# Mamba scan: in 8 of 16 steps VectorE adds the two states of the product and TensorE makes one identity sum instead of two

## What is computed

```python
dA = jnp.exp(delta[..., None] * -jnp.exp(a_log))
mi = ALPHA * delta[..., None] * Bm[:, :, None, :] * xb[..., None]

def scan_fn(carry, inp):
    h, v = carry
    dA_t, mi_t, C_t = inp
    v = BETA * v + mi_t
    h = dA_t * h + v
    y_t = jnp.einsum('ben,bn->be', h, C_t)
    return ((h, v), y_t)
...
y = ys.transpose(1, 0, 2) + dp * xb
y = y * jax.nn.silu(z)
return jnp.einsum('ble,de->bld', y, ow)
```

## Time and profile before

| | |
|---|---|
| median of 3 runs | 4198.9 us |
| the profiled execution, its own time | 4208.4 us |
| its span, first to last instruction | 4206.7 us |
| TensorE busy, share of the span | 3402.9 us, 81% |
| VectorE busy | 2586.9 us, 61% |
| GpSimd busy | 2097.3 us, 50% |
| ScalarE busy | 1958.7 us, 47% |
| L912 products on GpSimd, 512 | 1233.8 us, 2413 ns each |
| L1049 scans on VectorE, 512 | 1169.1 us, 2283 ns each |
| L1323 identity sums on TensorE, 2048 records | 1056.9 us |

### The profile page before, as it was taken

The page is one execution under the profiler, slowest core; times in us unless marked ns, Lnnn a source line. Parts: engine busy times, 40 slices in busy tenths (PEclk is TensorE's granted clock), DMA queues, the critical chain, the costliest instruction groups (busy, mean ns, idle before and its releaser), DMA issues. The chain is left out here.

```text
span 4206.7 us, 66615 instructions
## 1 busy us (share of the span) xinstructions
PE 3402.9 (81%) x20348; PEld 2295.0 (55%) x20349; DVE 2586.9 (61%) x3839; ACT 1958.7 (47%) x4228; POOL 2097.3 (50%) x1304
## 2 busy tenths in 40 slices
PE   6888886982899898999974998999989863799980
PEld 4455554651555555555543555555555543688870
DVE  3444442234677777777754777777777757654545
ACT  1211111212676767676734766676676733233320
POOL 0101100002677777777752877777777855321216
PEclk9888887995999999999986999999999985699995
DMA  1000000001222222222221222223232324111113
GB/s 53 0 0 0 0 0 22 0 30 53 54 67 68 65 69 63 70 63 69 63 61 32 73 63 63 71 55 81 54 80 53 79 72 168 61 45 47 47 43 109
DMA packets 151434, 227.93 MB, mean 54 GB/s; under 512 B 25108, under 2 KB 83892, under 8 KB 149558
## 3 DMA queue, kind: packets, MB, share of 16 engines
q1 hardware_dynamic: 143156, 202.30, 17.9%
q0 software_dynamic: 8064, 23.08, 1.8%
HBM read 119.99 MB, written 23.59 MB: 34 GB/s over the span
## 5 line engine op out<-in xcount | busy, mean ns | idle before, releaser
L912 POOL TENSOR_TENSOR m_hc<-m_h,m_Cb 128x1024 f32<-128x1024 f32 x512 | 1233.8, 2413 | 419.3 <-PE m_bank L1323 280.6
L1049 DVE TENSOR_TENSOR_SCAN m_h<-m_dA,m_vel 128x1024 f32<-128x1024 f32 x512 | 1169.1, 2283 | 59.4 <-ACT m_dA L1189 13.0
L1323 PE MATMUL m_bank<-m_hc,ident 128*128 128x512 f32 x2048 | 1056.9, 631 | 102.3 <-POOL m_hc L912 101.9
L1189 ACT ACTIVATE m_dA<-m_delta,m_rate 128x255 f32<-128x255 f32 x2048 | 874.0, 497 | 42.8 <-DVE m_h L1049 23.7
L1339 PE MATMUL m_vel<-m_M,m_U 128*128 128x128 bf16 x4096 | 544.9, 223 | 88.3 <-DVE m_h L1049 63.1
L1341 PE MATMUL m_vel<-m_M,m_U 112*128 112x128 bf16 x4096 | 545.1, 223 | 0.0
L1323 PEld LDWEIGHTS m_bank<-m_hc,ident 128*128 128x128 f32 x2048 | 362.4, 198 | 321.1 <-issue 221.3
L1339 PEld LDWEIGHTS m_vel<-m_M,m_U 128*128 128x128 bf16 x4096 | 403.2, 99 | 222.8 <-DVE m_h L1049 110.2
L1341 PEld LDWEIGHTS m_vel<-m_M,m_U 112*128 112x128 bf16 x4096 | 407.9, 100 | 81.0 <-issue 68.3
L1038 DVE TENSOR_TENSOR m_vel<-m_vel,m_entry 128x4 f32<-128x4 f32 x512 | 82.8, 162 | 377.1 <-PE m_vel L1341 375.3
L1253 PE MATMUL m_bank<-m_pair,m_in 128*128 128x256 f32 x1024 | 280.0, 402 | 37.6 <-DVE m_cv L989 31.8
(11 more groups left out here) (280 smaller groups left out, 5744.6 us busy)
## 6 DMA issues: line engine op xcount, KB each, us to landing
m_Cb<-m_c_rows SPq DMA_DIRECT2D x256, 256.0 KB, 3.3
m_M<-m_Mhi SPq DMA_DIRECT2D x128, 256.0 KB, 4.3
m_M<-m_Mlo SPq DMA_DIRECT2D x64, 256.0 KB, 3.9
m_U<-m_Uhi SPq DMA_DIRECT2D x128, 128.0 KB, 3.2
y_rows<-x_y SPq DMA_DIRECT2D x40, 256.0 KB, 2.1
m_U<-m_Ulo SPq DMA_DIRECT2D x64, 128.0 KB, 3.3
g_stage<-in_e_w SPq DMA_DIRECT2D x8, 1024.0 KB, 5.3
o_stage<-in_e_w SPq DMA_DIRECT2D x16, 512.0 KB, 4.4
```

Of the source, the lines that this page charges most:

```text
L912: nc.gpsimd.tensor_tensor(hc[:, g].rearrange("p m a t -> p m (a t)"), h[:, p % 2, 2 * g:2 * g + 2].rearrange("p m a t -> p m (a t)"), Cb[: ...
L1049: nc.vector.tensor_tensor_scan(flat(h), flat(dA), VB[:, 2 * g * 512:2 * (g + 1) * 512], 0.0, ALU.mult, ALU.add).then_inc(s["scan_done"], 1)
L1189: nc.scalar.activation(dA[:, p % 2, m, a, 1:CM], delta[:, par, m, 1:CM], ACT.Exp, scale=rate[:, m, NG * p + a:NG * p + a + 1]).then_inc(s[ ...
L1323: last = nc.tensor.matmul(Y[g][:], net.ident[:], hc[:, g, :, a, :], start=(p == 0 and a == 0), stop=(p == NPAIR - 1 and a == NG - 1))
```

## The change

In steps 2, 3, 4, 7, 8, 11, 12 and 13 of each chunk (`FOLDED`) VectorE adds the second state's half of `hc` to the first's, in place (`fold`, a `tensor_tensor` of 128x512 float32 with both inputs and the output in SBUF). TensorE then makes one identity matmul of the result instead of two. The fold of step k-2 stands behind the scan of step k on VectorE; it waits for product k-2. The one sum stands at the place of the second of the two before, and waits for the fold. The other eight steps stay as they are, among them the first two and the last two, which open and close the accumulation in PSUM. Over 32 chunks there are 256 folds.

```diff
+FOLDED = (2, 3, 4, 7, 8, 11, 12, 13)
+folds = lambda k: sum(f < k for f in FOLDED)
...
+                def fold(c, k):
+                    g = k % 2
+                    dve.wait_ge(s["hc_done"], 1 + AHEAD + c * NS + k + 1)
+                    nc.vector.tensor_tensor(hc[:, g, :, 0, :], hc[:, g, :, 0, :], hc[:, g, :, 1, :], ALU.add
+                                            ).then_inc(s["fold_done"], 1)
+
                 def slots(c, par, more, more2):
                     restart()
                     for at in range(HALF):
                         k = at // 2
                         if at % 2 == 0:
                             scan(c, k)
+                            if k - 2 in FOLDED:
+                                fold(c, k - 2)
...
                 def accumulate(c, k, a):
                     p, g = k // 2, k % 2
+                    if k in FOLDED:
+                        if a == 1:
+                            pe.wait_ge(s["fold_done"], 1 + c * len(FOLDED) + folds(k) + 1)
+                            pe.sem_inc(net.carrier, 1)
+                            nc.tensor.matmul(Y[g][:], net.ident[:], hc[:, g, :, 0, :], start=False, stop=False
+                                             ).then_inc(s["acc_done"], 1)
+                        return
                     if a == 0:
                         pe.wait_ge(s["hc_done"], 1 + AHEAD + c * NS + k + 1)
```

More of the change, by code:

```diff
@@ L714, in mamba_phase @@
                  "v_psum da_done scan_done hlast_done hc_done acc_done y_psum gated_done out_psum xm_done rate_done "
-                 "floor_done const_done first_in first_done entry_done fix_done c_kept c_spread0 c_spread1").split()
+                 "floor_done const_done first_in first_done entry_done fix_done c_kept c_spread0 c_spread1 fold_done").split()
         plain = ("loaded", "own_dve")
```

## The result

The changed kernel takes 4433.8 us (median of 4 runs, 4429.7 to 4444.6), the kernel before beside it 4199.2 us: a ratio of 1.056 (95% interval 1.054 to 1.058), 5.6% slower. The forecast was 4420 us.

What follows compares the result with a forecast made beforehand. TensorE was taken as the bound, but its gain would be lost waiting for folds: 6.1 us from the walk plus 0.8 from the clock, 6.9 us x 32 chunks = +221 us, on the median 4420 us; range 4285 to 4550.

Steps and rivals of the forecast that it cites:

- TensorE is the bound; its gain is 7 us in a chunk at most: Mamba layers: TensorE, 91% busy, bounds the kernel; 256 fewer identity sums give at most 230 us, 7 in a chunk.
- A fold by itself costs 0.69 us: On VectorE with GpSimd idle, a 128x512 float32 addition takes 0.69 us; eight make 5.5 us in a chunk.
- A fold waits for the GpSimd instruction that runs, and the next one waits for it: With two SBUF inputs on VectorE, a fold costs up to 3.04 us behind a product that has just begun.
- On who goes first: Between VectorE and GpSimd, whoever issues first holds the SBUF ports for the whole instruction; one row differed.
- My added 65 us for folds passed by a later product: If a later GpSimd product can pass a fold, one case per chunk adds about 2 us, 65 us in all.
- The walk, +6.1 us: One chunk followed with folds put into its before-times: 3.7 us by scan 13 plus 2.4 from folds 11 to 13.
- The clock, +0.8: TensorE falls to 1.2 GHz after idling around fold 7: +0.8 us in a chunk, bounds 0 and 2.5.
- The sum: Walk and clock together: 6.9 us in each of 32 chunks, +221 us, giving 4420 us.
- The signs: Profile after: folds mean 1.5 to 2.5 us, TensorE under 80% busy, longest fold wait about 10, chunks 77 to 79.
- The first rival: No port is shared, so a fold always costs 0.69 us: -2.8 us in a chunk, 4109 us; chance 0.12.
- my split of the 6.1 us: Waits for GpSimd on the chain add up to 10.3 us and move a chunk from -2.8 to +6.1 us.
- The turning point of 0.4 us a fold: The change turns from faster to slower where waits for GpSimd reach 3.3 us in a chunk, 0.4 a fold.

Runs made afterwards that it cites:

- e3: The changed kernel without any fold, the one sum waiting for the product alone (second state left out of 8 steps): 4130.5 us, ratio 0.984.
- e2: The changed kernel with each fold replaced by an operation of the same 512 elements, place and waits, one input in PSUM: 4220.3 us, ratio 1.004.
- e4: The kernel before plus eight additions per chunk with two SBUF inputs, behind the same scans as the folds, that nothing waits for: 4381.0 us, ratio 1.043.
- e12: The kernel before plus eight one-input reductions per chunk, behind the same scans as the folds, that nothing waits for: 4207.5 us, ratio 1.0015.
- e6: The change with folds in steps 7 and 8 only: 4297.2 us, ratio 1.021 against the kernel before.
- e7: The change with folds in steps 11, 12 and 13 only: 4282.9 us, ratio 1.018 against the kernel before.
- e5: The changed kernel with velocities of step 6 computed twice and of step 10 eight times, keeping TensorE busy during waits: 4409.5 us, ratio 1.048.
- e8: The change with folds in steps 2 and 10 only: 4155.3 us, ratio 0.989 against the kernel before.

## Why the prediction was right, point by point

- *TensorE is the bound; its gain is 7 us in a chunk at most.* The removed work is there (200 us less busy), but e3 shows that only 2.2 of the 7 us could be had. I read 91% busy as "the bound" too readily; another chain was about 2 us behind it. e3's waits point at scans and at the carries, but no run takes these apart.
- *A fold by itself costs 0.69 us.* The minimum is 665 ns; e2's stand-in has 668.
- *A fold waits for the GpSimd instruction that runs, and the next one waits for it.* Right, shown by the durations of the changed kernel and by the pairs of the changed kernel with e2 and of e4 with e12. The mean of 1.94 us is inside the 1.5 to 2.5 that I named.
- *On who goes first*, the Trainium skill ("SBUF — State Buffer", "Who interferes with whom") gives the ports to the one that issued first. By the recorded starts 35 of the 256 folds, 28 of them fold 8, went ahead of a product that had started 22 to 30 ns before them. The others that met a running GpSimd instruction had started 52 ns or more behind it, and each ended 0.54 to 0.55 us behind its end. So the trace agrees but for starts that lie within 30 ns. My added 65 us for folds passed by a later product were not needed.
- *The walk, +6.1 us.* In the chunk shown scan 0 of the next chunk comes 6.56 us later than before, and every anchor is within 0.75 us of the walk. In the medians it is +3.95 at scan 10 (walk +3.7), +5.9 at scan 11 (+5.7), +5.2 at scan 13 (+3.7) and +7.3 at the end (+6.1). Two parts came about otherwise. Fold 8 mostly did not wait; scan 11 was late all the same, because the velocities of step 11 were, held up behind sum 7 and made at the lower clock. That the walk was so near at scan 11 is partly luck. And behind scan 11 the waits gave back 0.7 us, not 2. The walk's sizes for folds 7 and 8 and for folds 11 to 13 agree with e6 and e7.
- *The clock, +0.8.* e5: 24 to 30 us, 0.8 to 0.9 in a chunk, as a lower bound.
- *The sum*, +6.9 in a chunk: it was (4433.8 - 4199.2) / 32 = +7.3.
- *The signs.* Folds, products, scans, the clock and the length of the chunks (78.0 us in the mean) came as named. TensorE's busy share is 80.5% in the first layer's window, not under 80%, and 74.8% in the second; its longest wait for a fold is 8.6 us from 1300 to 2050 us, not 10.
- *The first rival* was wrong in its price, and so was my split of the 6.1 us. I had put a fold without the shared port at -2.8 us in a chunk and so the port at 8.9. e2 gives +0.6 and the port 213.5 / 32 = 6.7. The step that failed is TensorE's path in that walk: I let the velocities keep their times, or come earlier, and put the wait of a sum for its fold at nothing. In the medians of e2 scan 7 comes 1.0 us later than before (the rival's walk: 0.7 earlier), scan 11 2.4 later, scan 13 2.3 later (1.1 earlier) and the next scan 0 1.0 later (2.8 earlier). So nearly all of the miss is there at scan 13. The velocities of step 7 stand behind sum 3, those of step 11 behind sum 7. Each of these sums now waits for an operation behind the very scan that the velocities wait for, so operation and sum come between that scan and the velocities; TensorE's waits for them are the 287.1 us above, and part of the work behind them ran at the lower clock. The forecast's own walk left the same out and is off by less, 1.5 us at scan 13 and 1.2 at the end; no run shows why by less.
- *The turning point of 0.4 us a fold* fell with it: e2 has no waits for GpSimd and is still not faster.

## What to carry to other kernels

Before work is moved to VectorE, look at where its inputs lie: an operation with two SBUF inputs is priced by the GpSimd instruction beside it, not by its own length, and one with an input in PSUM, or with one input, is not. Place it where VectorE waits anyway, as in e8; there even a fold of 2.8 us was off the path in most chunks. And when an engine at 91% is relieved, ask what the second longest chain is before counting the relief: here two folds, in steps 2 and 10 (e8, 44 to 50 us), gave more than half of what the eight of the change could have given at no price (e3, 70 us).

And look at what stands behind the receiver of such a result in its own stream. Here the sum that waits for the fold stands ahead of velocities; that held TensorE for 287.1 us even with an operation of 0.67 us (e2).

## What the runs showed of the hardware that I had not expected

- A one-input reduction of the same 512 elements costs 648 ns beside a busy GpSimd (e12), a two-input addition 1713 ns (e4) with 652 ns at best; both have 32 partitions, so a small operation waits as well.
- An unchanged line can get shorter by a third when the schedule around it shifts: L1003, 2315 to 1550 ns.
- With TensorE at work for 91% of the first layer's window the granted clock is 0.97; taking 7 us of its work out of a chunk, with no fold added, already lowers it to 0.94 at 85% (e3). In the window of the second layer it is 0.93 in both. How much time that costs no run shows.
- A two-input operation of VectorE ends 0.54 to 0.55 us behind the end of the GpSimd instruction that it waits for, 220 of 220 times in the changed kernel, though it takes 0.67 to 0.69 us by itself.
